# Scores and their maxima in mixed waves of matmuls, maxima by head in three rotating banks, small products in a bank of their own

## The reference

```python
x = x + 0.5 * ffn(layernorm(x))     # x: 16 sequences x 256 tokens x 128
x = x + attn(layernorm(x))
x = x + 0.5 * ffn(layernorm(x))

# ffn: top-1 of 8 experts (128 -> 512 -> 128, relu) for each token
# attn: 16 heads of 8
q, k, v = (xn @ w.T).reshape(B, T, H, 8) for w in (wq, wk, wv)
q, k = rope(rms(q)), rope(rms(k))
scores = einsum('bhtd,bhsd->bhts', q, k) / sqrt(8) + 1.0
y = einsum('bhts,bhsd->bhtd', softmax(scores), v)
return y.reshape(B, T, 128) @ wproj.T
```

## Time and profile before

| | |
|---|---|
| time, median of 3 | 597.53 us (594.77 to 598.96) |
| the profiled execution | 599.49 us, of it span 597.6 us |
| experts, first time, with all before it | 0 to about 147 us |
| attention, n = -20 to -1 | about 147 to 181 us |
| attention, n = 0 to 72 | 181 to 434 us |
| routing and experts, second time | 434 to 597.6 us |
| busy over the span | PE 83%, DVE 61%, ACT 61%, POOL 49% |

### The profile page before, as it was taken

The page is one execution under the profiler, slowest core; times in us unless marked ns, Lnnn a source line. Parts: engine busy times, 40 slices in busy tenths (PEclk is TensorE's granted clock), DMA queues, the critical chain, the costliest instruction groups (busy, mean ns, idle before and its releaser), DMA issues.

```text
span 597.6 us, 13470 instructions
## 1 busy us (share of the span) xinstructions
PE 493.5 (83%) x4207; PEld 358.5 (60%) x4207; DVE 367.3 (61%) x902; ACT 365.5 (61%) x824; POOL 294.5 (49%) x398
## 2 busy tenths in 40 slices
PE   7977999996799999999999999987704967768592
PEld 6736999973445555555555555554303867657592
DVE  5284666644776788888888888875284434333341
ACT  3734667632535788888888888776683434444340
POOL 5006545406984676778665555200004466656552
PEclk9989999999955899999999999999955878898887
DMA  8953333211000000000000000000063111111100
GB/s 237 350 186 88 83 94 101 65 33 36 22 15 14 12 12 12 12 12 12 8 2 3 2 4 3 3 2 2 2 211 114 42 55 55 55 54 56 49 22 1
DMA packets 27205, 31.99 MB, mean 54 GB/s; under 512 B 5326, under 2 KB 23669, under 8 KB 26882
## 3 DMA queue, kind: packets, MB, share of 16 engines
q1 hardware_dynamic: 21122, 18.54, 9.6%
q0 software_dynamic: 6016, 12.60, 7.5%
HBM read 19.64 MB, written 13.50 MB: 55 GB/s over the span
## 4 chain that ended last, share of the span: by engine, by line
PE 66%; DVE 12%; issue 7%; ACT 6%; another core or an unknown queue 3%; DMA 2%; POOL 1%; ACTq 1%; POOLq 0%; SPq 0%; DVEq 0%
PE PS L525 15%; PE PS L538 11%; PE PS L654 10%; PE PS L617 9%; DVE Smax L1157 5%; PE PS L602 5%; PE PS L587 3%; PE PS L639 2%; PE PS L486 2%; PE PS L515 2%; ACT QkT L735 1%; PE PS L664 1%; DVE AtCol L1012 1%; ACT Pt L828 1%
## 5 line engine op out<-in xcount | busy, mean ns | idle before, releaser
L1157 DVE TENSOR_REDUCE Smax<-PS 128x4 f32<-128x1024 f32 x128 | 156.5, 1223 | 46.4 <-PE PS L617 44.0
L359 POOL DMA_INDIRECT Xs<-rows,TokI x78 | 79.1, 1014 | 150.5 <-DVE TokI L1030 103.3
L828 ACT ACTIVATE Pt<-PS 128x1024 f32<-128x1024 f32 x128 | 128.4, 1034 | 5.1 <-PE PS L639 4.4
L525 PE MATMUL PS<-Pt 128*128 128x128 f32 x624 | 98.6, 306 | 32.5 <-ACT Pt L735 26.6
L525 PEld LDWEIGHTS PS<-Pt 128*128 128x128 f32 x624 | 84.5, 210 | 40.0 <-ACT Pt L735 30.1
L784 ACT ACTIVATE Pt<-PS,Bs 128x128 f32<-128x128 f32 x156 | 48.7, 363 | 94.6 <-PE PS L525 61.2
L538 PE MATMUL PS<-W,Pt 128*128 x624 | 89.8, 290 | 0.3 <-issue 0.2
L1053 DVE TENSOR_SCALAR Pt<-PS,Bs 128x128 f32<-128x128 f32 x156 | 47.5, 346 | 62.0 <-PE PS L525 39.3
L538 PEld LDWEIGHTS PS<-W,Pt 128*128 128x128 f32 x624 | 82.0, 205 | 1.6 <-issue 0.8
L617 PE MATMUL PS<-QkT 24*128 24x256 f32 x512 | 65.7, 334 | 11.3 <-DVE Smax L1157 7.7
L617 PEld LDWEIGHTS PS<-QkT 24*128 24x128 f32 x512 | 41.7, 197 | 48.6 <-ACT Pt L828 17.3
(11 more groups left out here) (143 smaller groups left out, 691.0 us busy)
## 6 DMA issues: line engine op xcount, KB each, us to landing
rows<-XX SPq DMA_DIRECT2D x16, 512.0 KB, 4.4
mid<-Pt SPq DMA_DIRECT2D x39, 64.0 KB
XX<-x SPq DMA_DIRECT2D x8, 256.0 KB, 5.1
W<-w1T SPq DMA_DIRECT2D x1, 2048.0 KB, 7.7
W<-w2T SPq DMA_DIRECT2D x1, 2048.0 KB, 12.6
Xs<-rows,TokI POOLq DMA_INDIRECT x78
QkT<-NmaxT SPq DMA_DIRECT2D x64, 4.0 KB
out<-Pt,TokI POOLq DMA_INDIRECT x39
```

The lines of the kernel that those rows point to most:

```text
L359: pool.indirect_dma_start(Xs[:, u, :], None, rows, bass.IndirectOffsetOnAxis(ap=TokI[:, t:t + 1], axis=0), bounds_check=N_TILES * P - 1, o ...
L525: last = nc.tensor.matmul(PS[:, 2 + 2 * (n % 2) + c // 2, (c % 2) * P:(c % 2 + 1) * P], Ws[:, n % R_WS, c * P:(c + 1) * P], XsT[:, n % 2, ...
L828: nc.scalar.activation(Pt[:, m % 2, 2 * pair:2 * pair + 2, :, :].rearrange("p h c t -> p (h c t)"), PS[:, score_bank(m, pair):score_bank(m ...
L1157: nc.vector.tensor_reduce(Smax[:, b % 2, :, at:at + 33:32].rearrange("p t h -> p h t"), PS[:, max_bank(m, pair):max_bank(m, pair) + 2, :]. ...
```

## The change

- `wave(n, pair)` replaces `scores` and `max_scores`. It issues, in turn, a matmul of the scores of group n for the heads of `pair` and one of the maxima's scores for the heads of the other pair: of group n + 5 for `pair` 0, of group n + 6 for `pair` 1. PE does two waves an iteration, with `values` between them; the steps that come once for a sequence, and `qk_transpose`, stand behind the second.
- The scores have banks 4 and 5 alone, so the second wave waits for the first `exps` of its iteration, and the first wave of the next for the second. `exps` waits for each pair apart.
- The maxima's scores go, a head a bank, to banks 0, 1 and 2 in turn. `maxima` is two reductions of 128x512 where there was one of 128x1024; a wave waits until the first of the two before it is done.
- Bank 3 takes the small products (`filled3`, `emptied3`, `use3`), and bank 7 is left to `qk_transpose`, which runs 8 groups ahead and not 7.
- ACT copies YuT and QkT between the two exponentials and the small products behind the second. The first stage's transposed rows lie in `Sq`'s memory (`XT`).

```diff
-QKT_LEAD = 7
+QKT_LEAD = 8
...
-        def score_bank(m, pair):
-            return 4 if pair else 0 if m % 2 and group(m + MAX_LEAD) else 2
-        def max_bank(m, pair):
-            return 2 * ((m + pair) % 2)
...
+        S_BANK, M_BANKS = 4, 3
...
-            def max_scores(m, pair):
...
-            def scores(m):
...
+            def wave(n, pair):
+                other = 1 - pair
+                m = n + MAX_LEAD - other
+                if group(n):
+                    if pair == 0:
+                        pe.wait_ge(max_in[n % R_QK], 16 * (n // R_QK + 1))
+                    if 2 * n + pair:
+                        pe.wait_ge(exp_ready, 2 * n + pair)
+                if group(m):
+                    if other == 0:
+                        pe.wait_ge(emptied7, use7["qkT", m])
+                    if 4 * m + 2 * other > 1:
+                        pe.wait_ge(smax_ready, 4 * m + 2 * other - 1)
+                for c in range(SEQ_TILES):
+                    for i in range(2):
+                        if group(n):
+                            h = 2 * pair + i
+                            rows = slice(32 * h, 32 * h + SPLIT + 1)
+                            score = nc.tensor.matmul(PS[:, S_BANK + i, c * T:(c + 1) * T], ...)
+                        if group(m):
+                            h = 2 * other + i
+                            rows = slice(32 * h, 32 * h + SPLIT)
+                            largest = nc.tensor.matmul(PS[:, (GH * m + h) % M_BANKS, c * T:(c + 1) * T], ...)
...
             for n in range(FIRST, END):
                 fill(n)
-                if group(n):
-                    scores(n)
-                if group(n + MAX_LEAD):
-                    max_scores(n + MAX_LEAD, 0)
...
+                wave(n, 0)
+                if group(n - 1):
+                    values(n - 1)
+                wave(n, 1)
...
-                nc.vector.tensor_reduce(Smax[:, b % 2, :, at:at + 33:32].rearrange("p t h -> p h t"),
-                                        PS[:, max_bank(m, pair):max_bank(m, pair) + 2, :].rearrange("p h (t s) -> p h t s", s=T),
-                                        AX, ALU.max).then_inc(smax_ready, 1)
+                for h in (2 * pair, 2 * pair + 1):
+                    nc.vector.tensor_reduce(Smax[:, b % 2, :, 32 * h + g],
+                                            PS[:, (GH * m + h) % M_BANKS, :].rearrange("p (t s) -> p t s", s=T),
+                                            AX, ALU.max).then_inc(smax_ready, 1)
```

More of the change, by code:

```diff
@@ L603, in qk_transpose @@
                 last.then_inc(filled7, 1)
-            def max_scores(m, pair):
[L606 to L613, removed]
-                for tt in range(SEQ_TILES):
-                    for h in (2 * pair, 2 * pair + 1):
-                        rows = slice(32 * h, 32 * h + SPLIT)
-                        last = nc.tensor.matmul(PS[:, max_bank(m, pair) + h % 2, tt * T:(tt + 1) * T],
-                                                QkT[rows, m % R_QK, 0, tt * P:(tt + 1) * P],
-                                                QkT[rows, m % R_QK, 1, :], start=True, stop=True)
-                last.then_inc(smax_ps, 1)
@@ L644, in values, with max_transpose @@
+            def max_transpose(b):
+                pe.wait_ge(smax_ready, GH * N_GRP * (b + 1))
+                for tt in range(SEQ_TILES):
+                    last = nc.tensor.transpose(PS[:, 3, tt * P:(tt + 1) * P], Smax[:, b % 2, tt, :], I[:])
+                last.then_inc(filled3, 1)
             def values(m):
@@ L711, in _ @@
                     project(seq(n, -8))
-                if ("turn", n) in use7:
+                if ("turn", n) in use3:
                     turn(n)
-                if group(n - 1):
-                    values(n - 1)
-                if group(n + QKT_LEAD) and not group(n - 1):
+                if group(n + QKT_LEAD):
                     qk_transpose(n + QKT_LEAD)
-                if group(n + MAX_LEAD):
-                    max_scores(n + MAX_LEAD, 1)
-                if group(n + QKT_LEAD) and group(n - 1):
-                    qk_transpose(n + QKT_LEAD)
-                if seq(n, 16) >= 0:
-                    project_qkv(seq(n, 16), 0)
-                if seq(n, 14) >= 0:
-                    project_qkv(seq(n, 14), 1)
             totals(1)
@@ L749, in chunk_copy @@
                     act.wait_ge(logits_ps, c - 1)
-                copy(XnT[:, c % 2, :], PS[:, bank, :]).then_inc(xnT_ready, 1)
+                copy(XT[:, c % 2, :], PS[:, bank, :]).then_inc(xnT_ready, 1)
             def normalise_rows(k, c):
@@ L895, in _ @@
                     exps(n, 0)
+                if group(n - 1) and n % 2 == 0:
+                    yu_copy(n // 2 - 1)
+                if group(n - 1 + QKT_LEAD):
+                    qkT_copy(n - 1 + QKT_LEAD)
+                if group(n):
+                    exps(n, 1)
                 if seq(n, 2) >= 0:
                     max_copy(seq(n, 2))
-                if ("turn", n) in use7:
+                if ("turn", n) in use3:
                     turn_copy(n)
-                if group(n):
-                    exps(n, 1)
-                if group(n - 1) and n % 2 == 0:
-                    yu_copy(n // 2 - 1)
-                if group(n + QKT_LEAD):
-                    qkT_copy(n + QKT_LEAD)
                 if n in ROOT_AT:
@@ L1189, in _ @@
                     residual(seq(n, -8))
-                if group(n + MAX_LEAD):
-                    maxima(n + MAX_LEAD, 1)
                 if seq(n, 20) >= 0 and n != XN4_LATE - 2:
```

124 lines of the change are left out of this document (62 added, 62 removed).

## The result

The changed kernel takes 611.61 us (median; 609.19 to 613.78), the kernel before 598.25 beside it: ratio 1.0233, 95% interval 1.0165 to 1.0301. It is slower by 2.3%, outside the range. The profiled execution takes 609.19 with a span of 607.4; before 599.49 and 597.6. It is the fastest of the four, so what follows explains the 9.8 us between the two spans; the other 3.6 of the 13.4 us between the medians lie in executions without a trace.

A forecast was written before the change was run, and what follows sets the result against it. It took PE as nearest to a bound in the middle, PE-DVE hand-overs later, ACT last. Terms -0.4, -3.2, +3.2, +0.5 sum to 0.1 on 599.49, taken as nothing; the median lies 2.0 lower: 597.0, range 584 to 608.

The forecast's parts named there:

- the loop in the middle: Middle of the attention, n = 4 to 48: a sequence takes 15.6 us as now, about -0.4 in all.
- 0.5 for `xn`: Type 0 of the middle loop: xn holds DVE for 0.5 us behind residual, leaving DVE free at 3.39.
- legs: Middle loop, from one type's second wave to the next: 4.22, 4.08, 3.90 and 3.44 us.
- n = 0 to 4 and the start: Stretch before n = 0 and first four groups: +2.3 at n = 0, -1.8 for the groups, together +0.5 us.
- n = 48 to 58: Late attention, DVE free: 3.44 us a group, 34.4 against 37.6 us, so -3.2.
- n = 58 to 63: Last groups, no maxima left: 20.5 us at 3.44 a group, so +3.2.
- The serial wait: Each wave waits for the exponential before it: 1.72 us a wave, 3.44 a group, now paid once a group.
- in the last groups alone it costs 3: Part of the rival of a falling clock: if it falls in the last groups only, 3 us are lost.
- PE's saving: Rival: PE is the bound and its saving gets through, 14.6 us a sequence, -12, 585 us; chance 0.22.
- DVE throughout: Rival: DVE bounds the kernel throughout, two reductions take 1.38 us without overlap, 604 us; chance 0.14.
- The clock: Rival: TensorE's clock falls in one low stretch over six groups of the middle, losing 8 us, 608; chance 0.10.
- The waves pack: Denies a rival: mixed waves of eight don't pack, 0.67 and not 0.43 us a wave, 620 us; chance 0.03.

The follow-up runs named there:

- Rope apart: The changed kernel with the gathers one iteration earlier and GpSimd's rope made to wait for xn, which stays in type 0: 575.33 us, ratio 1.0052, fourth chip.
- xn off the path: The changed kernel with xn in type 2, not type 0: 606.15 us, first chip; 576.79, third; with gathers an iteration earlier too, 597.41, ratio 1.0023, first.
- the changed kernel again: The changed kernel once more, unaltered, on a third chip: 581.16 us, ratio 1.0154 to the kernel before.
- added matmuls: The changed kernel with four matmuls without use behind the second wave of each iteration from n = 58 to 67: 580.19 us, ratio 1.0123, fourth chip.
- tail edit: The changed kernel with the second pair's scores in banks 1 and 2 once no maxima are left, both waves ahead of the values: 576.13 us, ratio 1.0051, second chip.

## Why the prediction was wrong

**The step that failed** is "the loop in the middle": 15.6 us a sequence, "n = 4 to 48 gives 11 x 0 and about -0.4". It measured +8.0, and +4.6 on a chip without the lag. Three things are in it.

1. The term "0.5 for `xn`", read from the earlier trace rows, where nothing ran on GpSimd beside it. In the new order its start and that of the rope coincide, and it holds DVE 1.14. It lies on DVE's path of type 0, so it showed in full. Rope apart: 0.59 again and 15.31, 0.3 below the forecast. xn off the path: 15.00, which is the forecast loop less its 0.5, to 0.14. Each of the other three legs was right to 0.14. The Trainium skill has the rule, in SBUF — State Buffer, section "SBUF: two separate sides": DVE and GpSimd share one pair of ports under an exclusive lock, which a GpSimd instruction, or one of DVE that uses both ports (in a two-port mode, or with two inputs from SBUF), keeps to its end while the other engine waits. The trace agrees in part. Beside the rope `xn` ends at 308.60, just behind the first of the two multiplications of 0.41 that start at 308.11, and the reductions from PSUM keep their 684 ns beside all of it. But by the page the first to start gets the pair, and here `xn` starts 0.03 ahead and is the one that waits, while GpSimd's 0.74 stays as it is elsewhere; and no run shows which mode `xn` runs in. What the experiments show is the cost of the meeting, not its mechanism.
2. The gathers were not in the sum. The change moved them beside no new work by the code, but in time they shift the rope onto `sums`: +0.44 a sequence, some 2.6 us, on the chips without the lag.
3. On the first chip the lag behind a gather takes the place of that and costs 1.01 a sequence (16.95 against 15.94), which makes 3.3 us more in all (179.46 against 176.12). No row of before showed it in the attention; its experts had it (the wait for remote, 26.9 us), and I didn't read that stage.

**n = 0 to 4 and the start.** Forecast +0.5 for both, measured +0.2, and -1.3 on the other chip. Counted from wave to wave, as forecast, its terms were +2.3 for the start of n = 0 and -1.8 for the first groups; measured were +1.9 and -1.7, on the other chip +0.6 and -1.9.

**n = 48 to 58.** Forecast -3.2, measured -3.1 on both. **n = 58 to 63.** Forecast +3.2, measured +3.0, nearly all of it at the full clock: 3.32 us a group (422.89 to 426.21) against 3.44. The serial wait was the whole of it: separate banks bring back 3.3. But the clock falls within these groups in all ten profiles with this tail. Where it falls in their last 2 to 3 us, they take 19.6 to 19.7; in the last 5, 20.5; and in five of the ten it falls 17 to 18 us before their end, and they take 24.0 to 24.4. The prediction had "in the last groups alone it costs 3" as a rival's half; it costs 4.4.

**What was left out:** the steps behind the last exponential, +3.5 us, a term that the prediction put at nothing without a reason. `values`, `project`, `y_transpose` and `turn` now run at half the clock:

```profile
434.76 1.94 PE L651 MATMUL PS<-Pt,Vg 128*32 128x256 f32 x16 [0.50 <-ACT Pt L821]
436.62 1.28 PE L681 MATMUL PS<-Wp,YnT 128*128 128x136 f32 x4
```

(the changed kernel again, third chip; 1.07 and 0.73 at the full clock). In the kernel before the clock falls only 5 us behind the last exponential, and they run at the full one. With the clock held, and the added matmuls in the way, it is +2.2; how much of that they cost was not tried. The tail edit takes 2.7 off, and the 0.8 left are open.

**Sums that don't come out.** By the prediction's own slots PE's work before is 4 x (1.10 to 1.29, 1.00 and 0.50) and 3.67, so 14.1 to 14.8 us a sequence and not some 15, and what PE alone could give back is 1.0 to 1.7 us and not 2.5. The last groups' 20.5 less 14.6 and 2.8 is 3.1 and not 3.2, and four times 0.4 is 1.6 and not 1.8. None of these is what failed.

**The rivals.** PE's saving does not get through: DVE releases the second wave of type 1. DVE throughout at 604 was the right direction with the wrong cause: reductions were as dear as forecast, an instruction with a hindrance beside it was dearer. The clock did not fall in the middle of either profile of the changed kernel; with `xn` in type 2 it once did. The waves pack: their slot is 0.43. The forecast of "same" would have held with xn at 0.59 and the gathers elsewhere: 1.0052 was measured for that on the fourth chip, and 1.0023 on the first with `xn` off the path.

## What to carry to other kernels

A duration taken from the trace of before holds only beside the same neighbours: when a change reorders engines, look for each fp32 instruction of DVE from SBUF on the path at what GpSimd does at the new moment, and move one of the two if they meet. Add up the legs between like events and compare them with the forecast's, leg by leg: here one of four was too long, and it led to the cause. Where a kernel issues gathers, run it on more than one chip before a signal that comes late is put down to the kernel.

## What the runs showed of the hardware

- The same program takes 597 us on one chip (and 598 in the first comparison, whose traces show the same lag) and 572 to 573 on three others. Of 27.2 us between two profiles 25.9 lie in the second expert stage, where gathers run on GpSimd beside every step, PE's signals reach ACT and DVE up to 1.4 us late, and the granted clock is lower (0.90 against 1.00). In the attention a wave's signals were late (0.33 to 1.02 us, 0.04 to 0.08 elsewhere) only behind a gather that started within `values`. What does it, in the chip or in its state at that hour, stays open.
- TensorE's granted clock fell at different moments of the last groups with the same program: 2.4 us before their end in one execution and 17.5 in another (19.6 and 24.0 us for them). With added matmuls it stayed at 1.00 until after the last exponential. The total, 1.0123, is not told apart from the 1.0154 without them.
- Two equal `xn` instructions of 0.34 us take 0.82 to 0.86 and 0.44 beside the rope, and a 128x64 one 0.69 and not 0.20. GpSimd's multiplications keep their length.
